# Attention softmax in a fused block: odd steps take the row maximum first, the second norm's rows go to two steps, and VectorE makes the lower half of the softmax shares

## The reference

```python
q_hk = (hidden_q @ Wq.T).reshape(b, s, H, K)             # hidden_q = layernorm(x), H = 16
q_big = jnp.einsum('bshk,hkq->bshq', q_hk, w_kc_q)
kv_rope = kv_c * cos[None] + _rotate_half(kv_c) * sin[None]
q_r = jnp.einsum('bshq,hqr->bhsr', q_big, W_qr)          # r = 64
k_r = jnp.einsum('bld,hdr->bhlr', kv_rope, W_kr)
attn = jax.nn.softmax(jnp.einsum('bhsr,bhlr->bhsl', q_r, k_r), axis=-1)
ctx_c = jnp.einsum('bhsl,bld->bhsd', attn, kv_rope)
out = jnp.einsum('bshd,hkd->bshk', ctx_c, w_kc_kv).reshape(b, s, H * K) @ Wo.T
x = x + jnp.tanh(g_xattn[0]) * out
x = x + jnp.tanh(g_ffn[0]) * ffn(layernorm(x))
```

## Time and profile before

| | before |
|---|---|
| median of 3 runs | 2029.69 us (2027.64 to 2030.72) |
| the profiled execution | 2027.22 us, span 2025.4 us |
| granted TensorE clock, mean | 0.984 of full |
| busy, share of the span | TensorE matmul 95%, VectorE 43%, GpSimd 35%, ScalarE 33% |
| the attention | about the first 880 us of the span |

### The profile page before, as it was taken

How to read it: one execution, slowest core, us unless ns; L and a number is a source line. 1 busy time by engine, 2 the same in 40 slices (tenths; PEclk the granted TensorE clock), 3 DMA queues, 4 the chain that set the end, 5 groups by cost and what they waited for, 6 DMA issues and landing times.

```text
span 2025.4 us, 32045 instructions
## 1 busy us (share of the span) xinstructions
PE 1915.3 (95%) x11801; PEld 1070.0 (53%) x11972; DVE 871.0 (43%) x1674; ACT 666.0 (33%) x1905; POOL 715.9 (35%) x779
## 2 busy tenths in 40 slices
PE   7799999999999988899999999999999999999999
PEld 7455555555555555444445555555554444444444
DVE  5655555555555555446642222222223433233243
ACT  5655555555555555522012222222210000000000
POOL 5655555555555565610023333343302110110101
PEclk9899999999999999999999999999999999999999
DMA  9445544444444555451329999999943522221202
GB/s 297 115 102 102 102 102 99 105 102 102 102 102 102 110 123 117 102 137 46 106 65 203 235 248 222 213 219 218 207 101 125 114 73 49 77 83 27 78 19 86
DMA packets 427300, 250.01 MB, mean 123 GB/s; under 512 B 360369, under 2 KB 366257, under 8 KB 427185
## 3 DMA queue, kind: packets, MB, share of 16 engines
q1 hardware_dynamic: 415664, 210.61, 44.5%
q0 software_dynamic: 11520, 37.76, 6.7%
HBM read 113.02 MB, written 48.23 MB: 80 GB/s over the span
## 4 chain that ended last, share of the span: by engine, by line
PE 56%; DVE 14%; issue 11%; ACT 9%; POOL 6%; DMA 2%; SPq 1%; DVEq 0%; POOLq 0%; ACTq 0%
PE score L725 11%; PE o L815 8%; PE score L804 7%; PE p_bank L725 5%; PE m_bank L725 5%; PE o L737 5%; ACT arena L892 5%; DVE arena L1015 4%; PE p_bank L804 4%; PE m_bank L804 4%; PE c_bank L737 3%; PE t_bank L737 3%; DVE arena L1090 3%; POOL arena L1384 2%; DVE arena L1141 1%
## 5 line engine op out<-in xcount | busy, mean ns | idle before, releaser
L583 PE MATMUL o<-arena 128*128 128x512 bf16 x1473 | 338.9, 379 | 4.7 <-DVE arena L1015 1.0
L892 ACT ACTIVATE arena<-score,arena 128x128 f32<-128x128 f32 x512 | 181.5, 367 | 268.7 <-DVE arena L1090 268.7
L725 PE MATMUL score<-arena 128*128 128x512 bf16 x1037 | 235.9, 381 | 2.6 <-DMA arena<-xn_d 1.3
L583 PEld LDWEIGHTS o<-arena 128*128 128x128 bf16 x1536 | 150.3, 99 | 155.0 <-DVE arena L1015 1.7
L1379 POOL TENSOR_TENSOR arena<-arena 128x512 bf16<-128x512 f32 x128 | 150.2, 1174 | 208.7 <-ACT arena L845 206.0
L632 PE MATMUL p_bank<-arena 128*128 128x256 bf16 x1536 | 195.4, 288 | 0.9 <-DVE arena L1015 0.9
L725 PEld LDWEIGHTS score<-arena 128*128 128x128 bf16 x1056 | 103.7, 98 | 128.1 <-issue 3.1
L632 PEld LDWEIGHTS p_bank<-arena 128*128 128x128 bf16 x1536 | 153.7, 103 | 32.9 <-DVE arena L1015 1.6
L1470 POOL TENSOR_TENSOR arena<-arena 128x1088 bf16<-128x1088 f32 x32 | 71.9, 2248 | 274.9 <-ACT arena L922 274.9
L815 PE MATMUL o<-arena 128*128 128x512 bf16 (+1 forms) x681 | 160.0, 379 | 2.0
L1015 DVE TENSOR_TENSOR arena<-arena 128x512 bf16<-128x512 f32 (+2 forms) x219 | 152.4, 705 | 17.1 <-ACT arena L932 5.0
(11 more groups left out here) (161 smaller groups left out, 2739.8 us busy)
## 6 DMA issues: line engine op xcount, KB each, us to landing
xrow_d<-arena SPq DMA_DIRECT2D x80, 256.0 KB, 3.7
arena<-w_expert SPq DMA_DIRECT2D x32, 544.0 KB, 5.3
arena<-w_shared SPq DMA_DIRECT2D x22, 384.0 KB, 3.5
arena<-x SPq DMA_DIRECT2D x16, 512.0 KB, 4.1
arena<-x SPq DMA_DIRECT2D x32, 256.0 KB, 4.2
x_d<-arena SPq DMA_DIRECT2D x32, 256.0 KB, 2.4
xn_d<-arena SPq DMA_DIRECT2D x32, 256.0 KB, 2.2
arena<-x_d SPq DMA_DIRECT2D x8, 1024.0 KB, 6.5
```

The lines of the kernel that those rows point to most:

```text
L583: mm = pe.matmul(o_bank[b % 2][:, :], lhsT=cT[u % 2][:, a, h, :], rhs=M_w[:, w, head_of(hg, h), :], start=(hg == 0 and n == 0), stop=(hg = ...
L725: mm = pe.matmul(dst[:, :], lhsT=wsh[m][:, a, col:col + P], rhs=xs[g % 2][:, w, t, :], start=(n == 0), stop=(n == 3 * KT - 1))
L892: mm = act.activation(prob[:, u % 4, h, :], score_bank[u % 2][:, h * S:(h + 1) * S], ACT.Exp, bias=neg_max[:, u % 4, h:h + 1], accum_out=d ...
```

## The change

In odd steps VectorE takes the row maximum before `x1`. VectorE makes the lower half of the share of unit k+4, behind the reciprocal (and behind the row maximum in odd steps), and GpSimd no longer does. The two rows of the second norm are made in step 2 and step 3, in both ahead of the lower half of the piece, in place of both at the end of step 2.

```diff
@@ VectorE, step(k, it)
                 links(*((1,) if m == 0 else ()))
+                if k % 2 == 1:
+                    row_max(k + 6, it)
+                u = k + 4
+                if within(u, NU):
+                    wait(dve, share_hi, u + 1, 16, it)
+                    lower(share[u % 2][:, LO, :], prob[:, u % 4].rearrange("p h n -> p (h n)"),
+                          share[u % 2][:, HI, :]).then_inc(share_lo, 1)
                 if k % 4 == 3 and within(k // 4, NB):
...
                                              in1=x1[b % 4], op0=ALU.mult, op1=ALU.add).then_inc(x1_done, 1)
-                if k % 2 == 1:
-                    row_max(k + 6, it)
                 u = k + 2
...
                 if k % 2 == 0:
                     row_max(k + 6, it)
+                if m in (2, 3):
+                    norm_2(m - 2, g2, g1, it)
                 q = k + 12
...
                 if m == 1:
                     norm_1(g1, it)
-                if m == 2:
-                    norm_2(g2, g1, it)
...
-            def norm_2(g2, g1, it):
+            def norm_2(s, g2, g1, it):
                 if within(g2, NG):
+                    b = 2 * g2 + s
                     wait(dve, rsqrt_step, RSQRT_OPS * (g1 + 1), 2 * RSQRT_OPS, it)
-                    for s in range(2):
-                        b = 2 * g2 + s
-                        wait(dve, xn2_lo, b - 1, 4, it)
-                        wait(dve, l2_mm, b - 1, 4, it)
-                        dve.tensor_scalar(xn2[:, s, :], x1[b % 4], mean_var[:, s, 0:1], rstd[:, s:s + 1],
-                                          ALU.subtract, ALU.mult).then_inc(xn2_ready, 1)
+                    wait(dve, xn2_lo, b - 1, 4, it)
+                    wait(dve, l2_mm, b - 1, 4, it)
+                    dve.tensor_scalar(xn2[:, s, :], x1[b % 4], mean_var[:, s, 0:1], rstd[:, s:s + 1],
+                                      ALU.subtract, ALU.mult).then_inc(xn2_ready, 1)
@@ GpSimd, step(k, it)
-                u = k + 4
-                if within(u, NU):
-                    wait(pool, share_hi, u + 1, 16, it)
-                    pool.tensor_tensor(share[u % 2][:, LO, :], prob[:, u % 4].rearrange("p h n -> p (h n)"),
-                                       share[u % 2][:, HI, :], ALU.subtract).then_inc(share_lo, 1)
                 u = k + 5
```

## The result

The changed kernel takes 1972.82 us in the median, the kernel before 2028.93 us in the same runs. The ratio is 0.972 (95% interval 0.9701 to 0.9739), so it is 2.8% faster. The forecast was 1981 us. One of the four runs took 2847.61 us at a mean clock of 0.656 and is not in the ratio. The profiled execution took 1971.24 us (span 1969.4), 56.0 us less in the span than before.

A forecast was written before the change was run, and what follows sets the result against it. A serial VectorE-ScalarE chain was taken to set the attention group's period, stalling TensorE's score; terms of -2.35 us plus 1.56 us of slow clock a group gave 48.6 us in all, so 1981 us median, range 1955 to 2008 us.

The forecast's parts named there:

- Row maximum first: Steps 7 and 3: x1 moves from ahead of the row maximum into VectorE's wait for ScalarE, twice -0.63 us.
- Share subtraction in odd steps: Behind the row maximum, covered by VectorE's 2.05 us wait for the exponentials: zero, with 0.3 us to spare.
- Share subtraction in steps 4 and 6: Before the point where the chain becomes the limit: taken as zero, up to 0.61 + 0.93 us each if uncovered.
- rival D: Slower, 2040 us, chance 0.08: ScalarE's share half late in steps 2, 4, 6, GpSimd goes first, 0.93 us more each.
- Share subtraction in even steps: On the path ahead of context and row maximum: +1.54 us in step 0 (0.93 of it waiting), +0.61 in step 2.
- Short operations on VectorE: Four-number operations held by GpSimd: two fall to 0.16 us, -0.84 and -0.79 us; the step 0 pair gives -0.31 us.
- The second norm: Pair leaves the end of step 2, -1.8 us; first row free before step 2's piece, second +0.50 us in step 3.
- The clock: Attention groups: 1.56 us of slow clock after the 3.64 us stall, taken as gone with a stall of about 1.5 us.
- The busy times: Whole kernel: GpSimd's busy time falls by 148 us, VectorE's rises by 86 us plus holds.
- The sum: Ten steady periods 36.3 us, three later ones 10.8 us, the first period 1.5 us: 48.6 us in all.

The follow-up runs named there:

- no_rowmax: The changed kernel with x1 ahead of the row maximum and share subtraction again in odd steps: 1993.26 us, ratio 0.983.
- rowmax_only: The kernel before with only the row maximum put ahead of x1 in odd steps: 2014.14 us, ratio 0.993.
- share_ahead: The changed kernel with the share subtraction ahead of the four aggregates in step 0: 1961.19 us, ratio 0.9663.
- share_late: The changed kernel with the share subtraction behind the row maximum in even steps too: 1949.28 us, ratio 0.9611.
- no_share: The changed kernel with the share subtraction back on GpSimd: 1972.1 us, ratio 0.9716.
- no_normsplit: The changed kernel with both rows of the second norm back at the end of step 2: 1987.8 us, ratio 0.9794.
- norm_only: The kernel before with only the second norm's rows split over steps 2 and 3, ahead of the piece: 1989.08 us, ratio 0.9807.
- share_only: The kernel before with only the share subtraction moved to VectorE, behind the row maximum in odd steps: 2010.03 us, ratio 0.991.

## Why the prediction was right, and which term was too small

What the terms made of VectorE's place in a group, against the same points of the group at 369.97 us before, counted from the score of step 4 (the earlier trace rows against the rows above; the row maximum of step 0 started at 396.12 us before):

| point | before | after | difference | forecast |
|---|---|---|---|---|
| reciprocal, step 0 | 24.23 | 23.45 | -0.78 | -0.63 |
| row maximum, step 0 | 26.15 | 26.63 | +0.48 | +0.60 |
| reciprocal, step 2 | 37.36 | 36.23 | -1.13 | -1.03 |
| piece's lower half, step 3 | 48.38 | 45.89 | -2.49 | -2.35 |

**Row maximum first**: twice 0.63 us forecast, 1.23 us in no_rowmax and 1.10 in rowmax_only. Right.

**Share subtraction in odd steps**: zero, right; it is held (1.17 us at 395.27), and the context's lower half of step 3 still waits 0.30 us for ScalarE behind it (397.40), as much as the prediction had to spare.

**Share subtraction in steps 4 and 6**: zero, right. In step 6 VectorE stands 3.27 us waiting for ScalarE's upper half of the share and the subtraction is then drawn out to 0.91 us (365.17), as rival D feared for the other steps, but the lower half of the context behind it starts 13.43 us after the score of step 4, against 13.53 us before the change.

**Share subtraction in even steps**: 1.54 and 0.61 us forecast, 1.48 and 0.66 us long; share_ahead and share_late show that they were on the path. Right as a term; against a group without the subtraction step 0 is only 1.03 us longer (no_share).

**Short operations on VectorE**: 0.16 and 0.15 us as forecast; no_share shows the cause. The pair in step 0 gave 0.18 us, not 0.31: the second was held by a rotary term (GpSimd at 378.53).

**The second norm**: two rows of 0.54 us; right. That the move of the share takes a hold off this pair by itself was not seen, and it is why the parts do not add up.

**The clock**: the slow clock, in eight of the ten groups before, is in none after; right in the result. The reason given was only in part right. One stall of 1.88 us with full clock was taken as a bound. Stalls of 2.0 us in no_normsplit were followed by the slow clock in four of ten groups, and stalls of 2.34 us in norm_only in one. So the length of the stall alone does not tell, and that 1.6 us would be safe did not follow from one stall of 1.88.

**The busy times**: GpSimd's fell by 111.6 us (715.9 to 604.3) where 148 was forecast, and VectorE's rose by 76.8 (871.0 to 947.8) where it was 86 and more. The forecast counted the moved operations; it left out that GpSimd is now held too (1.40 us for 1.04 at 389.05), and for VectorE the holds that went.

**The sum** was 48.6 us and the span fell by 56.0. The ten steady groups gave 504.82 - 466.88 = 37.9 us (forecast 36.3): 24.8 from the chain, 12.8 from the clock, and 0.3 because the periods after differ by some hundredths. The first period gave 47.13 - 44.62 = 2.5 us (1.5). The part that was mis-sized is the last three groups: 15.5 us instead of 10.8 (154.94 to 139.45 us). There GpSimd also splits feed-forward weights. In one of these groups of the kernel before, VectorE and GpSimd had

```profile
768.31 3.22 DVE L1141 TENSOR_SCALAR arena<-arena 128x512 f32<-128x512 f32 x2
```

```profile
768.31 1.64 POOL L1442 TENSOR_TENSOR arena<-arena 128x768 bf16<-128x768 f32 x1 [3.92 <-ACT arena L914]
769.91 1.34 POOL L1379 TENSOR_TENSOR arena<-arena 128x512 bf16<-128x512 f32 x1
```

The pair of the second norm was held for two GpSimd operations, 3.22 us, and the stall behind it was 5.02 us, 1.38 longer than in the steady groups. The pair took 3.22 us in the group ahead as well, and 2.31 in the last. In the changed kernel both rows are made in other places, at 0.54 us each:

```profile
718.53 0.54 DVE L1145 TENSOR_SCALAR arena<-arena 128x512 f32<-128x512 f32 x1
...
725.88 0.54 DVE L1145 TENSOR_SCALAR arena<-arena 128x512 f32<-128x512 f32 x1
```

So the same term, -1.80 + 0.50 = -1.3 us in the prediction, was worth -3.22 + 0.54 = -2.7 us in two of the three groups. no_normsplit confirms it: with the pair back at the end of step 2 it takes 2.38, 2.39 and 2.32 us there. The slow clock was in all three groups and went too. Windows of the same group before and after:

```profile
723.66:776.34 52.68, 46.77 (x357) 29.02 (x361) 28.25 (x59) 30.23 (x101) 33.37 (x34) 0.95 0.52 123
```

```profile
679.26:727.16 47.90, 45.21 (x357) 28.18 (x361) 32.29 (x67) 30.21 (x100) 27.59 (x25) 1.00 0.62 135
```

The longer pair makes 2.8 us of the 4.7 us that the forecast missed here; the rest was not taken apart further. The first score compared came 1.6 us later after the change and the rest of the program took 1.65 us less; these two were not looked into.

## What to carry to other kernels

When two engines hand work back and forth, look for the place in the list of the engine on the path where it waits for its partner, and put everything there that nobody needs soon. The same subtraction stood on the path with 1.48 and 0.66 us ahead of the row maximum; behind it, in the wait, the period was 1.35 us shorter and TensorE the limit in step 0, and that one move gave another 23.5 us (1972.8 to 1949.3) where the whole change had given 56. Test the parts of a change one by one, out of it and alone: here the move of the share gave 19 us alone (2029.09 to 2010.03) and nothing beside the other two.

## What the runs showed of the hardware that was not expected

How often the slow clock follows a stall depends on more than its length. Of ten steady groups it followed in 8 with stalls of 3.64 us (before), in 7 with 2.98 (rowmax_only), in 4 with 2.80 (share_only), in 1 and in 2 with 2.34 (norm_only, no_rowmax), in 4 with 2.0 (no_normsplit), and in none with 1.69 us or less. The kernel with the shorter stall of 2.0 us lost more to the clock, 6.0 us in ten groups, than the two with 2.34 us, 1.5 and 3.4. These counts are from one trace of each kernel; the mean clocks of the other runs agree for two of them, 0.986 to 0.991 in no_normsplit and 0.992 to 0.994 in norm_only. What decides was not tested.

VectorE gets in between two operations of GpSimd that follow each other without a gap. In the changed kernel the subtraction at 376.38 was held by the rescaling and ended at 377.86. The rotary term at 377.28, right behind the rescaling, was held by it in turn and took 1.17 us, where the other rotary terms of that size took 0.67 to 0.73.
